# Attention values of a fused Perceiver layer as three fp16 products instead of one f32 product, with parts of the step table moved

## The reference

```python
def _L0_xattn_ref(x, latents, mask, ln_x_g, ln_x_b, ln_l_g, ln_l_b, Wq, Wkv, Wout, ln_o_g, ln_o_b):
    ...
    xn = layernorm(x, ln_x_g, ln_x_b)
    ln = layernorm(latents, ln_l_g, ln_l_b)
    q = ln @ Wq
    kv_input = jnp.concatenate((xn, ln), axis=1)
    kv = kv_input @ Wkv
    k, v = jnp.split(kv, 2, axis=-1)
    ...
    sim = jnp.einsum('bhid,bhjd->bhij', q, k)
    sim = jnp.where(mask_full[:, None, None, :], sim, max_neg)
    attn = jax.nn.softmax(sim.astype(jnp.float32), axis=-1).astype(sim.dtype)
    out = jnp.einsum('bhij,bhjd->bhid', attn, v)
    ...
x = x + _L0_xattn_ref(ctx_1024, _layernorm(x, axis=-1), mask_BxS2_bk0, ...)
x = x + _L0_attn_ref(_layernorm(x, axis=-1), ...)
x = x + _L0_ffn_ref(_layernorm(x, axis=-1), ...)
```

## Time and profile before

| | us |
|---|---|
| median of 3 runs | 898.39 |
| lowest and highest of them | 897.13, 900.92 |
| the profiled execution, its own time | 900.01 |
| its span in the trace | 898.0 |
| mean granted PE clock over the span | 0.963 of 2.4 GHz |

### The profile page before, as it was taken

One profiled execution on the slowest core, in us unless ns is written; L12 is line 12 of the kernel. 1 busy time (PEld: TensorE's weight loads), 2 busy tenths in 40 slices (PEclk: granted clock), 3 DMA queues, 4 the chain that ended last, 5 costly groups with the idle time before them and its releaser, 6 DMA issues.

```text
span 898.0 us, 20741 instructions
## 1 busy us (share of the span) xinstructions
PE 832.3 (93%) x6742; PEld 445.9 (50%) x6743; DVE 594.8 (66%) x1515; ACT 450.5 (50%) x757; POOL 186.5 (21%) x354
## 2 busy tenths in 40 slices
PE   5699999999999999999999999999999999999753
PEld 4344544545454555545454545545454645455522
DVE  5777666666657576766657566766666576747577
ACT  5365454546465545546464545545465554443242
POOL 3011021212122221212222221211222222212101
PEclk9799999999999999999999999999999999999655
DMA  6113221111212121111212111201212111110001
GB/s 204 34 41 103 80 56 40 37 55 52 58 40 54 51 55 54 46 29 52 58 40 55 50 55 55 55 20 52 58 41 59 49 53 53 40 41 17 4 1 47
DMA packets 98347, 45.82 MB, mean 51 GB/s; under 512 B 72100, under 2 KB 90376, under 8 KB 98184
## 3 DMA queue, kind: packets, MB, share of 16 engines
q1 hardware_dynamic: 98256, 45.34, 18.2%
q10 hardware_dynamic: 56, 0.05, 0.0%
HBM read 25.69 MB, written 3.26 MB: 32 GB/s over the span
## 4 chain that ended last, share of the span: by engine, by line
PE 71%; DVE 17%; issue 6%; ACT 3%; DMA 1%; DVEq 1%; POOL 1%; ACTq 0%; SPq 0%; POOLq 0%
PE bank L1299 20%; PE bank L1353 7%; PE bank L1272 6%; PE bank L1227 5%; PE bank L1274 4%; PE bank L1276 4%; DVE mx L1694 4%; PE bank L1244 4%; PE bank L1370 3%; PE bank L1414 3%; DVE xf_all L1723 3%; PE bank L1389 2%; PE bank L1399 2%; PE bank L1243 2%; ACT arena L971 1%
## 5 line engine op out<-in xcount | busy, mean ns | idle before, releaser
L986 ACT ACTIVATE p<-bank,maskbias 128x512 f32<-128x512 f32 x224 | 154.2, 688 | 232.6 <-PE bank L1276 231.1
L1299 PE MATMUL bank<-p,xv 128*128 128x512 f32 (+1 forms) x512 | 238.0, 616 | 0.3 <-POOL arena L840 0.3
L1694 DVE TENSOR_REDUCE mx<-bank 128x1 f32<-128x512 f32 x256 | 165.5, 682 | 53.2 <-PE bank L1244 52.8
L1690 DVE TENSOR_TENSOR qkl_l<-bank,qkl_h 128x512 f16<-128x512 f32 x64 | 41.1, 685 | 76.7 <-ACT qkl_h L974 76.7
L1299 PEld LDWEIGHTS bank<-p,xv 128*128 128x128 f32 (+1 forms) x512 | 74.9, 188 | 31.5 <-issue 23.8
L1272 PE MATMUL bank<-qkc_h,xtT_h 128*128 128x512 f16 (+1 forms) x256 | 86.9, 389 | 0.0
L1244 PE MATMUL bank<-xtT_h,qkc_h 128*128 128x448 f16 x256 | 86.7, 358 | 0.0
L1274 PE MATMUL bank<-qkc_l,xtT_h 128*128 128x512 f16 (+1 forms) x256 | 85.0, 379 | 0.0
L1276 PE MATMUL bank<-qkc_h,xtT_l 128*128 128x512 f16 (+1 forms) x256 | 85.0, 379 | 0.0
L1243 PEld LDWEIGHTS bank<-ltT,qkl_h 128*128 128x128 f16 x256 | 24.9, 97 | 95.4 <-DVE mx L1694 53.9
L1353 PE MATMUL bank<-arena,wvF 128*64 128x128 f32 x1024 | 69.3, 278 | 0.0
(11 more groups left out here) (260 smaller groups left out, 1461.1 us busy)
## 6 DMA issues: line engine op xcount, KB each, us to landing
arena<-den_dram SPq DMA_DIRECT2D x62, 128.0 KB, 3.2
qkc_h<-arena SPq DMA_DIRECT2D x30, 256.0 KB, 2.4
qkc_l<-arena SPq DMA_DIRECT2D x30, 256.0 KB, 2.4
raw<-in_ctx SPq DMA_DIRECT2D x32, 192.0 KB, 2.5
raw<-in_ctx SPq DMA_DIRECT2D x64, 32.0 KB, 2.2
lt<-lt_dram SPq DMA_DIRECT2D x60, 31.8 KB, 2.1
arena<-in_L_xattn_Wkv SPq DMA_DIRECT2D x1, 1024.0 KB, 6.7
ltT_dram<-x_all SPq DMA_DIRECT2D x4, 256.0 KB, 3.5
```

Of the source, the lines that this page charges most:

```text
L986: a.activation(p32[0:r, slot, :], sbank[t % SRING][0:r, :], ACT.Exp, bias=bias).then_inc(s_probs_ready, 1)
L1299: op = mm(bk[:, :], rows_of[at, :], p32[at, slot, :], start=tile < 2, stop=tile in (0, plan.TILES - 1))
L1694: v.tensor_reduce(mx[:, hq_tile, part:part + 1], bk[:, 0:width], AX.X, ALU.max).then_inc(s_jobs_taken, 1)
```

## The change

Values of all 16 steps of a pair are made of fp16 halves. `p32`'s four slots hold two fp16 halves of 512 numbers each, `xv` and `lt` hold high and low halves of the rows. ACT writes the exponential twice from the same bank: to fp16 (the high half), then in f32 to one of two new buffers `p_all`, for which it waits until GpSimd has finished with it. GpSimd subtracts the high half from it and writes the low half (`low_probs`, one step later in its queue). PE then does low rows by high probabilities, high rows by high, high rows by low. The context's halves come from one copy to fp16 and one subtraction on GpSimd, the latents' from one ACT copy and one GpSimd subtraction per block of four pairs; they are stored to DRAM and loaded as halves.

Moved: RSTD and MASK one step later, RDEN of the second half pair from 3 to 5, MOVE from 8 to 11, XB, SHIFT, EXP, P1, P2, SC, KEXP by one, X1B by two, ALIBI by one and two; EXP now stands right behind the exponentials of its step. Blocks 1 to 3 of the latents are prepared over more steps of the first two pairs. `rden_rows` is cut in two: the store, and `rden_spread`, which comes in the next half pair for the first batch of a pair and behind `load_rows` for the other. The sum of the two denominator columns is a reduction instead of an addition.

```diff
-LATE = dict(wv=[0, 1, 2, 4], lt=[None, 6, 8, 14], aw=[7])
-BLOCK_AT = {1: (1, 2, 7), 2: (7, 8, 9), 3: (9, 14, 15)}
-ALIBI_AT = 15
+LATE = dict(wv=[0, 1, 2, 4], lt=[None, 6, 10, 17], aw=[7])
+BLOCK_AT = {1: (1, 4, 7), 2: (7, 8, 11), 3: (9, 14, 17)}
+HALVES_AT = {1: (6, 7), 2: (9, 10), 3: (15, 16)}
+ALIBI_AT = 18
...
-    STATS={4: (0, 4)}, AGGR=4, RSTD=4, XHAT=6, MASK=6,
+WINDOW = Plan(N - 448, ({0, 1, 2, 3, 4}, {0, 1, 2, 3, 4}), dict(
+    STATS={4: (0, 4)}, AGGR=4, RSTD=5, XHAT=6, MASK=7,
     START=dict(QP=[-3, -3], QC=[-2, -2], QL=[-1, -1], T=[-2.5], MAX=[1, 1, 2, 2, 3, 3, 4, 4], MT=5),
     ODD=dict(T=[0], MAX=[2.5, 3, 3, 3.5, 4, 4, 4.5, 5], MT=6),
     NEXT=dict(QP=[0, 0.5], QC=[1.5, 6.5], QL=[8.5, 9.5]),
     EVEN=dict(T=[7.5], MAX=[10.5, 11, 11, 11.5, 12, 12, 12.5, 13], MT=14), XV={2: (0, 4)},
-    RDEN=3, MOVE=8, ST1=[3, 4, 5, 6], YN=[6, 7], XB=7, ST2=8, M0=9, P0=9, X1=10, X1B=15, M1=10, P1=10,
-    XH=12, XHT=13, XHT_OUT=13, QKV=14, QKV_OUT=14, VBLK=15, KEXP=15, SC=16, ALIBI=[17, 18], SMAX=22, SHIFT=22, EXP=23,
-    PT=[24, 25], PT_OUT=[24, 25], PV=26, CX=27, CXT=28, CXT_OUT=28, WO=29, X2=30, P2=30, XF=31))
+    RDEN=(3, 5), MOVE=11, ST1=[3, 4, 5, 6], YN=[6, 7], XB=8, ST2=8, M0=9, P0=9, X1=10, X1B=17, M1=10, P1=11,
+    XH=12, XHT=13, XHT_OUT=13, QKV=14, QKV_OUT=14, VBLK=15, KEXP=16, SC=17, ALIBI=[18, 20], SMAX=22, SHIFT=23, EXP=24,
+    PT=[24, 25], PT_OUT=[24, 25], PV=26, CX=27, CXT=28, CXT_OUT=28, WO=29, X2=30, P2=31, XF=31))
...
-                    sp.dma_start(lt[M * half:M * half + M, par, 0:127], lt_dram[cols_of, 0:127]).then_inc(s_lat_loaded[par], 16)
+                    sp.dma_start(lt[M * half:M * half + M, par, :, :].rearrange("p h d -> p (h d)"), lt_dram[cols_of, :]).then_inc(s_lt_loaded[par], 16)
...
                 sp.dma_start(den_dram[par, :].rearrange("(p c) -> p c", p=P), rcol[:, :]).then_inc(s_den_stored, 16)
+
+            def rden_spread(b, par):
+
                 sp.wait_ge(s_den_stored, 16 * b + 16)
...
-                if j == 0:
-                    sp.wait_ge(s_setup_dve, setup_done("lt", 0))
-                else:
+                sp.wait_ge(s_lat_lo, j + 1)
+                sp.dma_start(lt_dram[512 * j:512 * j + 512, :].rearrange("(a p) d -> p a d", p=P),
+                             lat_halves[:, block_of(j), :, :].rearrange("p a h d -> p a (h d)")).then_inc(s_lat_stored, 16)
+                if j > 0:
                     sp.wait_ge(*late_done("lt", j))
+                    store_transposed(j)
+
+            def store_transposed(j):
...
+                            rden_spread(b - 2, par)
...
-                        if since or k == 1:
+                        if since and k == 0:
                             rden_rows(b - 1, 1 - par, pair)
-                        if since and k == 0:
+                            rden_spread(b - 1, 1 - par)
                             load_x(i - 1)
+                        if more and k == 1:
+                            load_rows(plan, i, last, 1 - par)
+                        if k == 1:
+                            rden_rows(b - 1, 1 - par, pair)
                         if not since and k == 1:
                             store_block(1)
                             store_block(2)
                         if since == 1 and k == 0:
                             store_block(3)
-                        if more:
+                        if k == 0:
                             load_rows(plan, i, last, 1 - par)
...
+
+            def latents_low(j):
+
+                pool.wait_ge(s_lat_hi, j + 1)
+                g.tensor_tensor(lat_halves[:, block_of(j), 1, :], lat[:, block_of(j), :], lat_halves[:, block_of(j), 0, :], ALU.subtract).then_inc(s_lat_lo, 1)
+
+            def low_probs(plan, i, k, t):
+
+                if (k, t) in plan.SPLIT:
+                    r, slot, made = plan.rows(t), slot_of(plan, k, t), plan.halves_made(i, k, t)
+                    pool.wait_ge(s_probs_ready, (i * 2 + k) * plan.STEPS + t + 1)
+                    g.tensor_tensor(p_halves[0:r, slot, 1, :], p_all[0:r, (plan.halves_made(0, k, t) - 1) % 2, :], p_halves[0:r, slot, 0, :], ALU.subtract).then_inc(s_p_lo, 1)
 
             def ahead(plan, n, par, t):
 
...
+                    if first < c1:
+                        assert halved == list(range(first, c1))
+                        g.tensor_copy(xv_halves[:, par, first:c1, 0, 0:127], raw[:, par, first:c1, 0:127]).then_inc(s_xv_hi[par], 1)
+                    if first > c0:
+                        op = g.tensor_copy(xv[:, par, c0:first, 0:127], raw[:, par, c0:first, 0:127])
+                    if first < c1:
+                        pool.wait_ge(s_xv_hi[par], (n - par) // 2 + 1 if isinstance(n, int) else (n - par + 2) // 2)
+                        op = g.tensor_tensor(xv_halves[:, par, first:c1, 1, 0:127], raw[:, par, first:c1, 0:127], xv_halves[:, par, first:c1, 0, 0:127], ALU.subtract)
                     if c1 == CH:
                         op.then_inc(s_xv_ready, 1)
...
                         k, t = divmod(s, plan.STEPS)
+                        if t > 0:
+                            low_probs(plan, i, k, t - 1)
+                        elif since or k == 1:
+                            low_probs(plan, i - 1 + k, 1 - k, plan.STEPS - 1)
                         if not (last and k == 1):
                             prep(plan, i * 2 + k + 1, 1 - k, t)
                         if not last:
                             ahead(plan, i * 2 + k + 2, k, t)
                         background(plan, i, since, s, tail)
-                        if not since:
-                            late_weights(s)
...
+
+                act.wait_ge(s_lhat_ready, j + 1)
+                a.activation(lat_halves[:, block_of(j), 0, :], lat[:, block_of(j), :], ACT.Copy).then_inc(s_lat_hi, 1)
 
             def setup(plan):
...
-                a.activation(p32[0:r, slot, :], sbank[t % SRING][0:r, :], ACT.Exp, bias=bias).then_inc(s_probs_ready, 1)
+                if (k, t) in plan.SPLIT:
+                    made = plan.halves_made(i, k, t)
+                    a.activation(p_halves[0:r, slot, 0, :], sbank[t % SRING][0:r, :], ACT.Exp, bias=bias)
+                    if happened(made - 2):
+                        act.wait_ge(s_p_lo, made - 2)
+                    a.activation(p_all[0:r, (plan.halves_made(0, k, t) - 1) % 2, :], sbank[t % SRING][0:r, :], ACT.Exp, bias=bias).then_inc(s_probs_ready, 1)
+                else:
+                    a.activation(p32[0:r, slot, :], sbank[t % SRING][0:r, :], ACT.Exp, bias=bias).then_inc(s_probs_ready, 1)
 
             def copy_context_part(plan, b, pair, k, h):
...
                             move_latents(i)
                         prep(plan, i, last, s + 0.5)
                         background(plan, i, since, s, tail)
-                        if not since:
-                            late_weights(s)
+                        if since < 2:
+                            late_weights(s + 2 * plan.STEPS * since)
 
...
                 tile, half = plan.steps[t]
                 slot = slot_of(plan, k, t)
-                pe.wait_ge(s_probs_ready, b * plan.STEPS + t + 1)
+                split = (k, t) in plan.SPLIT
+                if split:
+                    pe.wait_ge(s_p_lo, plan.halves_made(i, k, t))
+                else:
+                    pe.wait_ge(s_probs_ready, b * plan.STEPS + t + 1)
                 halves = (0, 1) if half is None else (half,)
+                if t == 0:
...
                 c = plan.chunk(tile)
-                rows_of = lt[:, k, :] if tile == 0 else xv[:, k, c, :]
-                for bk, at in parts:
-                    op = mm(bk[:, :], rows_of[at, :], p32[at, slot, :], start=tile < 2, stop=tile in (0, plan.TILES - 1))
+                last = tile in (0, plan.TILES - 1)
+                if split:
+                    halves_of = lt[:, k, :, :] if tile == 0 else xv_halves[:, k, c, :, :]
+                    for n, (row, prob) in enumerate(((1, 0), (0, 0), (0, 1))):
+                        for bk, at in parts:
+                            op = mm(bk[:, :], halves_of[at, row, :], p_halves[at, slot, prob, :], start=tile < 2 and n == 0, stop=last and n == 2)
+                else:
+                    for bk, at in parts:
+                        op = mm(bk[:, :], xv[at, k, c, :], p32[at, slot, :], start=tile < 2, stop=last)
                 op.then_inc(s_values_done, 1)
...
-                if t == plan.at["RDEN"]:
+            def normalise(plan, b, k, t):
+
+                if t == plan.at["RDEN"][k]:
                     dve.wait_ge(s_den_col, 32 * b + 32)
                     if happened(b):
                         dve.wait_ge(s_den_stored, 16 * b)
-                    v.tensor_tensor(rcol[:, :], dcol[:, 0, :], dcol[:, 1, :], ALU.add).then_inc(s_dsum_ready, 1)
+                    v.tensor_reduce(rcol[:, :], dcol[:, :, :].rearrange("p z c -> p c z"), AX.X, ALU.add).then_inc(s_dsum_ready, 1)
                     dve.wait_ge(s_dsum_ready, b + 1)
```

118 lines of the change are left out of this document (78 added, 40 removed).

## The result

The changed kernel took **868.75 us** (median, 867.28 to 870.95), the kernel before 899.24 us beside it: a ratio of 0.9668, 95% interval 0.9637 to 0.9698, or 30 us less. Forecast: 866, range 843 to 886. The number was met, but in part by luck: two of its terms were off by some 12 and 15 us with opposite signs.

A forecast was written before the change was run, and what follows sets the result against it. TensorE was taken to bound the kernel; gains of 1.24 and 1.15 us less 0.2 for the port make 2.2 a pair, x 15.5 = 34, less 2 for start and end: 32 off 898.4, so 866 us, range 843 to 886.

The forecast's parts named there:

- What bounds it: Whole kernel: TensorE, busy 832.3 of 898.0 us; its time in a pair of 50.05 us is what counts.
- TensorE's saving, 3.7 us a pair, of which 2.4 arrive: Values products of all 16 steps: 12 save 0.21 us, 4 save 0.30; waits let only 1.24 and 1.15 through.
- Steps 0 to 3: Start of a pair: second exponential delays the second queries, so 0.64 us is gained where products alone give 1.0.
- Steps 4 to 7: Rest of first half: steps 4 to 6 give 0.21 us each, step 7 nothing; 0.6 in all.
- Steps 8 to 15: Second half: ScalarE's queue full in steps 8 to 10, then VectorE paces; 1.15 us gained of 1.9.
- Moved roots and denominators at 0, bounds 0.2: GpSimd's roots, SP's reciprocal store and spreading: moving them costs nothing, bounds minus 0.2 to plus 0.2 us a pair.
- The shared port at 0.2: SBUF side shared by GpSimd and VectorE: differences cost normalisations 0.2 us a pair, bounds minus 0.3 and 9 x 1.08 = 9.7.
- Start and end at 2 us, bounds 0 and 4: Latents' block preparation priced 0, the last step's longer chain not overlapped: 2 us lost over the run.
- late blocks stand wider apart: 0: Latents' blocks: one extra copy and difference each fall in steps where both engines idle, so cost 0.
- The sum: Whole run: 2.2 us a pair x 15.5 = 34, less 2 for start and end: 32 us gained.
- all arrives: Rival: waits at steps 1, 7 and 13 do not come about, the full 3.7 us a pair arrives; 843 us, chance 0.15.
- The port's rivals: VectorE's nine instructions meet GpSimd's differences: at random, 887 us, chance 0.09; or regularly, 937 us, chance 0.06.

The follow-up runs named there:

- the run with the moves alone: Changed kernel with the 14 context steps of a pair back to f32 values, all moves and the latents' halves kept: 889.94 us, ratio 0.9884.
- the second exponential over 64 columns: Changed kernel with the second exponential made over 64 of 512 columns, the difference in full: 869.94 us, ratio 0.9667.
- the short differences: Changed kernel with GpSimd's difference of probabilities over 64 of 512 columns, other low parts left at 0: 864.85 us, ratio 0.9607.
- the last version: Changed kernel with block 3 and ALiBi table moved, queries fetched a batch ahead, last pair's scales and roundings a step earlier, transposes a step later: 865.83 us.
- both 64-column edits: Changed kernel with both the second exponential and the difference over 64 of 512 columns: 854.99 us, ratio 0.9501.
- the combined kernel: Changed kernel with every pair's queries fetched a batch ahead, block 3's halves a step later, last pair's weight transposes a step later: 865.45 us, ratio 0.9612.
- The two repaired kernels: The combined kernel and the last version, both edits of the changed kernel around pair 1 and the last pair: 865.45 and 865.83 us.

## Why the prediction was right, point by point

- **What bounds it**: right. TensorE 90% busy, and no run found another bound of the steady pair.
- **TensorE's saving, 3.7 us a pair, of which 2.4 arrive**: the single product is right (TensorE's timeline below: a full values step is 0.65 us, 457.90 to 458.55), but not the share that arrives: of the 2.99 us the moves bring 0.5 or more. The 14 context products save 3.1 and gave 1.87.

```profile
457.90 0.81 PE L1399 MATMUL bank<-p,xv 128*128 128x512 f16 x3
458.55 0.19 PE L1333 MATMUL bank<-ltT,qkl_h 128*128 128x64 f16 x1
```

- **Sizes**: difference 1.17 us (taken 1.08), GpSimd 31.8 us a pair (30), ScalarE 34.6 (36.3), period 47.06 (47.8).
- **Steps 0 to 3**: 0.96 us gained (0.64). The second exponential costs 0.68 in steps 0 and 3, more than the 0.36 of the walk. In the run with the moves alone these steps gained 0.70, 0.30 of it from the latents' products, so the moves give back some 0.4.
- **Steps 4 to 7**: 0.44 us gained (0.6); step 7 gives nothing, as said.
- **Steps 8 to 15**: 1.59 us (1.15). ScalarE's full queue in steps 8 to 10 costs 0.04 us, as the second exponential over 64 columns shows. That VectorE paces from there is right: its run without a gap is there again, and TensorE waits at two places for what it delivers, 0.31 us in step 12 (457.67), as before the change, and 0.29 in step 14 (shown: VectorE's first maxima of the run and its last result, and TensorE):

```profile
455.24 1.29 DVE L1799 TENSOR_REDUCE mx<-bank 128x1 f32<-128x512 f32 x2 [0.69 <-PE bank L1334]
...
461.51 0.17 DVE L1802 TENSOR_REDUCE negm<-mx 128x8 f32<-128x8 f32 x1
...
461.82 0.27 PE L1337 MATMUL bank<-ident,negm 128*8 128x128 f32 x1 [0.29 <-DVE negm L1802]
```

  The run takes 6.44 us (before 6.73), since the sum and the reciprocal now stand behind it, and starts 0.87 us earlier in its half (walked: 0.75). That makes 1.16 us of gain where the walk had 0.75; the rest of the half gives 0.4, as walked. What was wrong is the price 0 of the moved denominators, not the pacing.
- **Moved roots and denominators at 0, bounds 0.2**: wrong. They are worth 0.67 and 0.51 us a pair, each by undoing it alone; together not tried. The text had the mechanism for the roots and then gave the move no price, since it costed the move against the kernel before, where no difference stood behind it. For the denominators it looked at SP's queue and at the reader of the reciprocals alone, and not at the 0.3 us that their making takes in VectorE's run nor at the 1.06 us copy on ScalarE; both now stand where TensorE does not wait for them. With the reciprocals back alone it was VectorE's wait for the fetch, with the maxima behind it.
- **The shared port at 0.2**: right for the steady pair (0.00), too low for the last one, which lost 4.9 us less when the differences were short (part of that is the clock's: step 14 took 2.60 us there). The context's normalisation kept under the 0.5 us that would have spoken against the forecast, with 0.439, but not near 0.32; and the slow `xf_all` was not freed: 1.07 us, against 0.34 with the short differences.
- **Start and end at 2 us, bounds 0 and 4**: wrong, and the largest miss. Had all 15.5 pairs gained 2.99 us, the span would be 46.3 us shorter; it is 28.8, so 17.5 were lost. Of these 11.0 stand in pair 1 (8.03 slower instead of 2.99 faster), 4.7 from the start of pair 15 on, and 1.8 ahead of pair 1 and in pair 2. In pair 1 "late blocks stand wider apart: 0" failed: the walk did not follow the SP queue past the stores of blocks 1 and 2, nor VectorE's list past block 3 and the table. It had costed the parted spreads and context loads on this queue, and not the queries' DMA behind the stores.
- **The sum**: steady gain 34 predicted, 46.3 measured (12 more); start and end 2 predicted, 17.5 measured (15 more). The two misses cancelled, which is luck: with pair 1 as in the last version (47.20 instead of 54.34) the time would have been some 7 us lower, about 862 (an estimate from these two numbers), for the same forecast.
- **The rivals**: "all arrives" gave a period of 46.4, and with both 64-column edits the run came to 46.36; but that period holds the moves too (0.67 and 0.51 us, if they add), so not all products arrive even then. Part of the rest is VectorE's pace in steps 12 to 14; how much, no run shows. The port's rivals were right on the mechanism and wrong on the place. Of the other signs, TensorE does wait before the second queries (0.37 us for xtT_l, at 421.88) and before the maxima.

What stays open: no run joined the repaired pair 1 (47.20) with the better last pair (9.18). From the starts of pair 15, 740.85, and the 119.6 us that the combined kernel takes from there, it would have a span of about 860 us; that is worked out, not run. Open too are which move gives step 3 its 0.4 us, what the moves are worth together, and why the clock differed behind the same wait. The two repaired kernels, 865.45 and 865.83 us, beat the kernel before by 3.9 and 3.7%; against the changed kernel (0.9637 to 0.9698) the first one's interval ends just below and the second's overlaps.

## What to carry to other kernels

When a transfer or a wait is moved, list every DMA queued behind it, also those that have nothing to do with the change, and the pair in which one-off work meets it. When a long wait stays after its named releaser is repaired, look for a second input that was late by as much; a variant in which the first is early makes the profile name the other. A move that looks free in the old kernel can be what makes the new one work, and half of a paired move can cost eight times what the whole one gives. A forecast that is met says little until its terms are measured one by one.

## What the runs showed of the hardware

- A VectorE tensor_scalar from and to SBUF that meets a 512-element difference on GpSimd ends only when that does: 0.23 becomes 1.06 us, four of them 1.94 instead of 1.09. Through this a shorter ScalarE instruction made the kernel's period 0.33 us longer, 0.86 lost in step 7 against 0.54 gained in others.
- GpSimd's f16 result from an f32 and an f16 input, 512 elements, takes 1.17 us; 1024 elements of f32 take 1.90.
- Behind waits of TensorE the granted clock stood between 0.50 (1.2 GHz) and 0.59: at 0.50 for 6 us behind two waits of 1.62 us, at 0.50 for 5 us behind one of 4.31 us, at 0.59 and 0.56 for 4 us behind one of 2.12 us. In another run it stayed at 1.00 behind the same 2.12 us wait. At 0.50 the scores' product takes 0.63 us instead of 0.38. The same wait cost 1.6 us more in one run than in the other.
- The queries' transfer of 64 KB landed 2.9 us after its issue behind the four stores of 256 KB, and 2.1 us after it when issued ahead of them.
